# A second head group whose exponentials VectorE transposes in 32x32 blocks and TensorE multiplies as 32x32 array tiles

## The reference, cut to what matters

```python
# layer 0, 8 heads of 32
q, k, v = proj(Wq, bq), proj(Wk, bk), proj(Wv, bv)
scores = einsum('bhqd,bhkd->bhqk', q, k) / sqrt(32)
scores = where(adj + eye > 0, scores, -inf)
out = einsum('bhqk,bhkd->bhqd', softmax(scores), v)
h = x + out @ Wo.T + bo
h = (h - mean(h)) * rsqrt(var(h) + 1e-5) * gamma + beta
# layer 1, one head, logits that are a sum of a row and a column term
fp = h @ fc_w.T + fc_b
logits = (fp @ q_w.T + q_b) + (fp @ k_w.T + k_b).T + (1 - adj) * -1e9
y = softmax(leaky_relu(logits)) @ fp + h
```

## Time and profile before

| | |
|---|---|
| time, median of 3 runs | 985.11 us (984.9 to 985.22) |
| the profiled execution | 985.61 us, of which its span 983.4 us |
| TensorE's granted clock, mean over the span | 0.981 |
| busy: PE, PEld, DVE, ACT, POOL | 95%, 79%, 78%, 81%, 31% |
| DMA: moved, mean rate | 112.59 MB, 114 GB/s |

### The profile page before, as it was taken

The page is one execution under the profiler, slowest core; times in us unless marked ns, Lnnn a source line. Parts: engine busy times, 40 slices in busy tenths (PEclk is TensorE's granted clock), DMA queues, the critical chain, the costliest instruction groups (busy, mean ns, idle before and its releaser), DMA issues. The chain is left out here.

```text
span 983.4 us, 22056 instructions
## 1 busy us (share of the span) xinstructions
PE 932.2 (95%) x7432; PEld 777.8 (79%) x7432; DVE 768.7 (78%) x2012; ACT 796.1 (81%) x1900; POOL 300.5 (31%) x408
## 2 busy tenths in 40 slices
PE   4498999999999999999999999999999999999966
PEld 3276888888888888888788888878887888888755
DVE  3287987979788797978878797888879797887832
ACT  2187988989888897988889798988989898897923
POOL 0002332334333233433214243432323343232441
PEclk8699999999999999999999999999999999999988
DMA  5576856666575666657476665737666564756100
GB/s 150 85 110 149 118 141 108 130 119 99 136 116 133 108 130 129 109 126 117 123 119 133 123 129 109 118 124 116 150 111 129 108 108 130 118 120 108 44 22 22
DMA packets 74430, 112.59 MB, mean 114 GB/s; under 512 B 6736, under 2 KB 33360, under 8 KB 74320
## 3 DMA queue, kind: packets, MB, share of 16 engines
q1 hardware_dynamic: 74320, 111.18, 58.8%
HBM read 52.44 MB, written 8.39 MB: 62 GB/s over the span
## 5 line engine op out<-in xcount | busy, mean ns | idle before, releaser
L912 DVE CUSTOM_DVE_ANT_0 sm_bank<-sm_bank,masks 128x512 f32<-128x512 f32 x512 | 352.3, 698 | 124.1 <-PE sm_bank L494 121.2
L679 ACT ACTIVATE e<-sm_bank,row_min 128x512 f32<-128x512 f32 x512 | 355.3, 696 | 41.9 <-DVE row_min L912 41.9
L504 PE MATMUL et_bank<-ident,e 128*128 128x128 f32 x2048 | 307.9, 272 | 3.2 <-DVE e_t L920 1.9
L504 PEld LDWEIGHTS et_bank<-ident,e 128*128 128x128 f32 x2048 | 251.6, 140 | 42.5 <-issue 7.3
L494 PE MATMUL sm_bank<-k_stack,q_stack 96*128 96x512 f32 x512 | 248.0, 485 | 13.5 <-DMA k_stack<-kt_lo 12.7
L671 ACT COPY e_t<-et_bank 128x512 f32<-128x512 f32 x272 | 161.0, 592 | 16.1 <-PE et_bank L504 14.2
L920 DVE COPY e_t<-et_bank 128x512 f32<-128x512 f32 x240 | 164.4, 685 | 11.8 <-PE et_bank L504 10.2
L494 PEld LDWEIGHTS sm_bank<-k_stack,q_stack 96*128 96x128 f32 x512 | 97.2, 190 | 43.5 <-issue 25.5
L443 PE MATMUL o_bank<-e_t,v 128*32 128x256 f32 x2048 | 123.8, 382 | 0.0
L476 PE MATMUL shared<-feat,z 128*128 128x256 f32 x512 | 121.6, 381 | 0.8 <-ACT z L621 0.8
L679 ACT ACTIVATION_READ_ACCUMULATOR e<-sm_bank,row_min 128x1 f32 x512 | 106.9, 209 | 0.0
(11 more groups left out here) (110 smaller groups left out, 1578.9 us busy)
## 6 DMA issues: line engine op xcount, KB each, us to landing
adj_in<-in_adj SPq DMA_DIRECT2D x32, 1024.0 KB, 5.3
q_stack<-qt_hi SPq DMA_DIRECT2D x64, 256.0 KB, 7.1
k_stack<-kt_hi SPq DMA_DIRECT2D x64, 256.0 KB, 7.2
x_in<-in_x SPq DMA_DIRECT2D x16, 512.0 KB, 6.4
q_stack<-qt_lo SPq DMA_DIRECT2D x32, 256.0 KB, 7.1
k_stack<-kt_lo SPq DMA_DIRECT2D x32, 256.0 KB, 11.1
h<-in_x SPq DMA_DIRECT2D x16, 512.0 KB, 3.9
out_y<-h SPq DMA_DIRECT2D x32, 256.0 KB, 6.8
```

Source lines behind the costliest of these rows:

```text
L504: last = nc.tensor.transpose(et_bank[n % TURNED][:, c * P:(c + 1) * P], e[:, n % ROOM, c * P:(c + 1) * P], ident[:, :])
L679: nc.scalar.activation(e[:, k, :], sm_bank[n % SCORED][:, :], ACT.Exp, scale=-1.0, bias=row_min[:, k:k + 1], accum_out=row_sum[:, g, qt, i ...
L912: nc.vector.tensor_tensor_reduce(bank[:, :], bank[:, :], mask[b % 2][:, qt * N:(qt + 1) * N], 1.0, -LOWEST, ALU.add, ALU.min, row_min[:, k ...
```

## The change

- The tiles of group 1 are no longer transposed on PE and copied from PSUM. `BLOCK` = 2 slots after its scores, DVE transposes each of them from `e` to `e_t` in blocks of 32x32 (`turn_blocks`, one instruction for 128x512). A block stays in its strip of 32 partitions: the strip then holds keys, and the 32 queries of the strip lie along the row.
- The products of group 1 (`pv2`, `pv3`) become `times_v_blocks`: 128 float32 products each, with 32 rows (keys), 32 columns (one head) and 128 moving columns. Each takes one 32x32 tile of the array, and eight consecutive ones take eight different tiles. The four query strips go to four banks: the two transpose banks, `o_bank` and one shared bank. Their key order needs v in every strip, so four transfers on SP's queue (`v4`, 256 KB each) spread it to `v_blocks` once a batch.
- `o_normal` of group 1 becomes four instructions of 128 columns. `turn` of a batch's first two tiles now waits for it.
- The mask (`make_mask`) and the normalising (`normal_rows`) go to GpSimd. `finish` is split: ACT divides by the row sum into `z`, GpSimd adds `z` to h.
- `TURN` goes from 3 to 4, `ROOM` from 4 to 6, DVE copies 4 of the remaining 16 transposed tiles and ACT 12. All tables and the order within a slot are new.

```diff
+HALF = TILES // NG
-TURN = 3
-ROOM = 4
+TURN = 4
+ROOM = 6
+BLOCK = 2
-DVE_COPIED = (0, 3, 5, 6, 13, 14, 15, 18, 22, 24, 25, 26, 27, 28, 29)
+DVE_COPIED = (0, 7, 8, 11)
...
 PE_AT = {
+    "at3": 64, "pv2": 33, "rb1": 35, "pv3": 36, "v1": 4, "xt0": -26, "op0": 39, "op1": 40, "xt1": -23, "k0": -21,
+    "q0": -20, "ht1": 46, "ht0": 46, "fc1": 48, "fc0": 49, "kb": 50, "pv0": 18, "v0": -11, "q1": -11, "pv1": 23,
+    "k1": -8, "et0": 56, "rb0": 25, "et1": 59, "at0": 59, "et2": 59, "at1": 61, "et3": 62, "at2": 63}
...
 DVE_AT = {
+    "rc1": 32, "o_n1": 36, "x_lo0": -26, "h_add0": 39, "stats0": 40, "h_add1": 40, "stats1": 40, "moments": 40,
+    "x_lo1": -23, "k_lo0": -20, "q_lo0": -19, "h_lo1": 46, "h_lo0": 46, "rc0": 17, "q_dot1": 49, "q_dot0": 49,
+    "l_max0": 50, "l_max1": 50, "q_lo1": -10, "k_lo1": -8, "l_recip": 60, "o_n0": 29}
...
 def tile(s):
-    return s // (TILES // NG), s // 2 % GH, 2 * (s // (TILES // PAIRS) % 2) + s % 2
+    if s < HALF:
+        return 0, s // 2 % GH, 2 * (s // (TILES // PAIRS)) + s % 2
+    return 1, (s - HALF) // NT, s % NT
...
+        v_blocks = sb("v_blocks", [P, NT, NT, P])
+        o_quarter = [*et_bank, o_bank, bank_of["pv2"]]
...
+            def spread_values(b):
+                sp.wait_ge(act_done.sem, act_done.all("v", b))
+                sp.wait_ge(pe_done.sem, pe_done.of("pv3", b - 1))
+                for quarter in range(GH):
+                    sp.dma_start(v_blocks[quarter * DH:(quarter + 1) * DH, :, :, :], v[:, :, P:2 * P]).then_inc(v_spread.sem, 16)
...
+            def times_v_blocks(half, b):
+                pe.wait_ge(blocks_turned.sem, blocks_turned.of((half + 3) * (TILES // PAIRS) - 1, b))
+                if half == 0:
+                    pe.wait_ge(v_spread.sem, v_spread.of("v4", b))
+                    pe.wait_ge(act_copied.sem, act_copied.of(max(u for u in range(HALF) if u not in DVE_COPIED), b))
+                    pe.wait_ge(dve_copied.sem, dve_copied.of(max(u for u in range(HALF) if u in DVE_COPIED), b))
+                    pe.wait_ge(dve_done.sem, dve_done.of("o_n0", b))
+                    pe.wait_ge(*bank_read("pv2", b))
+                blocks = e_t[:, half, :, :, :].rearrange("p k g n -> p (k g n)").rearrange("p (h q c n) -> p h q c n", h=2, q=NT, n=DH)
+                for kt in range(NT):
+                    for a in range(NT):
+                        for quarter in range(GH):
+                            rows_in = slice(quarter * DH, (quarter + 1) * DH)
+                            for j in range(2):
+                                o = (2 * half + j) * DH
+                                last = nc.tensor.matmul(
+                                    o_quarter[quarter][o:o + DH, 0:P].rearrange("d (q n) -> d q n", q=NT),
+                                    v_blocks[rows_in, a, kt, o:o + DH], blocks[rows_in, j, :, kt * NT + a, :],
+                                    start=(kt == 0 and a == 0), stop=(kt == NT - 1 and a == NT - 1))
...
             def turn(u, b):
                 pe.wait_ge(exp_done.sem, exp_done.of(u, b))
+                if u < TURNED:
+                    pe.wait_ge(dve_done.sem, dve_done.of("o_n1", b - 1))
...
+            def turn_blocks(u, b):
+                dve.wait_ge(exp_done.sem, exp_done.of(u, b))
+                dve.wait_ge(pe_done.sem, pe_done.of(f"pv{u // (TILES // PAIRS) - 2}", b))
+                nc.vector.transpose(blocks_to(u), e[:, (TILES * b + u) % ROOM, :].rearrange("p (t k a) -> p t a k", t=NT, a=NT))\
+                    .then_inc(blocks_turned.sem, 1)
...
+            def divide(half, b):
+                    last = nc.scalar.activation(z[:, c, 0:D], bank_of[f"at{c}"][:, k * D:(k + 1) * D], ACT.Identity,
+                                                scale=l_recip[:, c:c + 1])
...
+            def finish(half, b):
+                    last = nc.gpsimd.tensor_tensor(h[b % 2][:, c, :], h[b % 2][:, c, :], z[:, c, 0:D], ALU.add)
```

More of the change, by code:

```diff
@@ L124, in all @@
         return max(self.of(step, b) for step in self.place if step[:-1] == name and step[-1].isdigit())
-FILLS = [name for name, _ in steps(PE_AT) if not name.startswith("pv") and name not in ("at1", "at3")]
+FILLS = [name for name, _ in steps(PE_AT) if name not in ("pv0", "pv1", "pv3") and name not in ("at1", "at3")]
 BANK = {
-    "at2": 1, "k1": 0, "v0": 1, "op0": 0, "op1": 1, "v1": 1, "xt0": 1, "xt1": 0, "q0": 0, "ht0": 0, "ht1": 1, "k0": 1,
-    "fc0": 0, "fc1": 1, "kb": 0, "q1": 0, "et0": 0, "et1": 0, "at0": 0, "et2": 1, "et3": 0, "rb0": 1, "rb1": 1}
+    "at2": 0, "k1": 1, "v0": 0, "op0": 1, "op1": 0, "v1": 0, "xt0": 0, "xt1": 1, "q0": 0, "ht0": 0, "ht1": 1, "k0": 1,
+    "fc0": 0, "fc1": 1, "kb": 1, "q1": 1, "et0": 0, "et1": 1, "at0": 0, "pv2": 1, "et2": 1, "et3": 1, "rb0": 0, "rb1": 0}
 BANK["at1"], BANK["at3"] = BANK["at0"], BANK["at2"]
@@ L308, in iteration @@
                 for s in range(TILES):
+                    if (b := due(SP_AT, "store0", s, t)) is not None:
+                        store(0, b)
+                    if (b := due(SP_AT, "v4", s, t)) is not None:
+                        spread_values(b)
+                    if (b := due(SP_AT, "store1", s, t)) is not None:
+                        store(1, b)
+                    if (b := due(SP_AT, "x_again", s, t)) is not None:
+                        for half in range(2):
+                            sp.wait_ge(stored[half].sem, stored[half].of(f"store{half}", b - 2))
+                        sp.dma_start(h[b % 2][:, :, :], rows(x, b)).then_inc(h_loaded.sem, 16)
                     if (b := due(SP_AT, "adj", s, t)) is not None and b > 0:
-                        sp.wait_ge(dve_done.sem, max(dve_done.all("mask", b - 1), dve_done.all("l_max", b - 2)))
+                        sp.wait_ge(pool_done.sem, pool_done.all("mask", b - 1))
+                        sp.wait_ge(dve_done.sem, dve_done.all("l_max", b - 2))
                         sp.dma_start(adj_in[:, :, :], rows(adj, b)).then_inc(adj_loaded.sem, 16)
+                    if (b := due(SP_AT, "stack0", s, t)) is not None:
+                        stack(0, b)
                     if (b := due(SP_AT, "x", s, t)) is not None and b > 0:
@@ L319, in iteration @@
                         stack(1, b)
-                    if (b := due(SP_AT, "store1", s, t)) is not None:
-                        store(1, b)
-                    if (b := due(SP_AT, "store0", s, t)) is not None:
-                        store(0, b)
-                    if (b := due(SP_AT, "x_again", s, t)) is not None:
-                        for half in range(2):
-                            sp.wait_ge(stored[half].sem, stored[half].of(f"store{half}", b - 2))
-                        sp.dma_start(h[b % 2][:, :, :], rows(x, b)).then_inc(h_loaded.sem, 16)
-                    if (b := due(SP_AT, "stack0", s, t)) is not None:
-                        stack(0, b)
             sp.wait_ge(setup_pe, 7)
@@ L525, in iteration @@
+                    if (b := due(PE_AT, "q1", s, t)) is not None:
+                        project_qk("q", WQ, 1, b)
+                    if (b := due(PE_AT, "pv1", s, t)) is not None:
+                        times_v(1, b)
                     if (b := due(PE_AT, "k1", s, t)) is not None:
                         project_qk("k", WK, 1, b)
+                    u, off = ago(s, TURN)
+                    if on(t, off) and u < HALF:
+                        turn(u, t + off)
+                    if (b := due(PE_AT, "at3", s, t)) is not None:
+                        attend(3, b)
@@ L542, in iteration @@
                         fc_project(1, b)
[L543 to L551 removed]
+                    if (b := due(PE_AT, "pv0", s, t)) is not None:
+                        times_v(0, b)
@@ L657, in recips @@
                 copy(recip_wide[g][:, :], f"rb{g}", bank_of[f"rb{g}"][:, :], b)
-            def normal_rows(half, b):
-                act.wait_ge(pool_done.sem, pool_done.of("shift", b))
-                for c in range(2 * half, 2 * half + 2):
-                    last = nc.scalar.activation(h[b % 2][:, c, :], h[b % 2][:, c, :], ACT.Identity, bias=shift[:, c:c + 1],
-                                                scale=rstd[:, c:c + 1])
-                last.then_inc(act_done.sem, 1)
             def copy_turned(u, b):
@@ L686, in iteration @@
+                    u, off = ago(s, TURN)
+                    if on(t, off) and u < HALF and u not in DVE_COPIED:
+                        copy_turned(u, t + off)
+                    if (b := due(ACT_AT, "fin1", s, t)) is not None:
+                        divide(1, b)
                     if (b := due(ACT_AT, "x_hi0", s, t)) is not None:
@@ L968, in iteration @@
-                    if (b := due(DVE_AT, "moments", s, t)) is not None:
-                        combine(b)
                     if (b := due(DVE_AT, "k_lo0", s, t)) is not None:
@@ new lines, in iteration @@
+                    if (b := due(POOL_AT, "mask1", s, t)) is not None:
+                        make_mask(1, b)
```

(10 more changed lines are left out.)

441 lines of the change are left out of this document (225 added, 216 removed), and 24 rows, old and new, of tables (ACT_AT, DVE_AT, PE_AT, POOL_AT).

## The result

The changed kernel takes 1205.9 us (1198.8 to 1209.2), the kernel before 985.0 beside it: a ratio of 1.223 [1.217, 1.229]. The forecast was 946 us in a range of 934 to 1030, so sign and range are both wrong. The profiled execution took 1198.8 us with a span of 1197.1, at a mean granted clock of 0.922 (0.981 before).

The account below looks back on a forecast made before the run. PE was taken to set the pace: 56.7 - 7.0 + 3.6 = 53.3 us a period, plus 0.5 for unevenness; 15 periods 2.9 us shorter, plus 4 us at the ends, gave 946 us, range 934 to 1030.

Parts of the forecast that it names:

- The issuing need not bind: PE, `pv2` and `pv3`: 16 instructions must start every 0.109 us, 7 ns each; a burst showed under 5 ns each.
- rival 3: PE's instruction fetches too slow for 512 a step: about 1020 us at 6.4 us a step, 1240 at 13.8; chance 0.08.
- charged SP's queue with nothing: SP's queue: `v4` adds one MB a batch where 7 move, but `pv2` is 45 us away; no time charged.
- charge of 0.5 us for uneven work: DVE's work falls unevenly over the slots against PE's: 0.5 us a period, ends 0 and 2.
- Eight tiles side by side, rounds of 0.109 us, a step of 3.5: PE, `pv2` and `pv3`: 32 rounds each, 3.75 us with edges in place of 1.95, +3.6 us a batch.
- Rival 1: PE, `pv2` and `pv3`: small tiles run four, not eight, at a time; period 60.3 us, 1043 us in all; chance 0.08.
- rival 2: PE: a floor between starts of products, 0.027 us, makes a step 6.9 us; 1032 us in all; chance 0.07.
- 16 tiles of transposes gone, 7.0 us: PE: 16 tiles of four transposes removed, 0.436 us a tile, 7.0 us less a batch.
- DVE's transpose at 0.60: DVE: each of 16 block transposes a batch costs 0.60 us as a copy does, 9.6 in all; bounds 0.35 and 1.15.
- rival 4: DVE's transpose slow, or DVE otherwise the bound: at 1.15 us each DVE has 56.8 us, up to 1010 us in all; chance 0.12.
- Masks on GpSimd at 1.4 each: GpSimd: two masks of 1024 columns a batch at about 1.4 us each, 2.8 us, on the least loaded engine.
- The ends, +4: After the last scores nothing overlaps: longer `pv3`, `o_n1`, last division and addition, and normalising add 4 us.

Follow-up runs that it names:

- later stacks: The changed kernel with SP's transfers of group 1's stacks waiting for the last step of products (`pv3`) of the batch before: 1104.2 us, ratio 1.120.
- short products: The changed kernel with 32 moving columns instead of 128 in each new product: 1218.5 us; with SP's stack transfers also made to wait, 1124.4 us.
- plain copy: DVE's block transpose replaced by a copy of the same 512 elements, in the changed kernel with half the products and SP's stack transfers delayed: 961.0 us.

## Why the prediction was wrong

**The step that failed** is the one in the change on PE that read "The issuing need not bind", and took 3.75 us from "what the burst and the independent strips show". It asked how close instructions can start and not how fast they are brought. It was named as rival 3, *Instructions do not arrive fast enough*, with 0.08. Its upper price, 1240 us, is near the result by another working: not a steady 27 ns each, but 13.6 ns each from block to block (the steps with later stacks: 5.4 and 6.0 us; the rival had 6.4 from "3 us" a fetch), plus one pause a batch of 5 to 9 us, for a fetch that stands behind 1.5 MB of stack transfers. The rival's lower price, about 1020, left out the second. But with the stacks later, and the steps no longer than it said, the time was 1104 and not 1020; the rest is in the sum below. That a fetch could stand behind the stacks was in view: the page gave 62 packets for 240 instructions each, and the changed table puts `stack1` at the end of an iteration (it waits for the last scores), with `pv2` at slot 1 of the next. I had charged SP's queue with nothing, because I asked only whether its own transfers land in time.

The Trainium skill bears on it in "Runtime: NRT & Kernel Launch", section "Instruction fetch mechanics": PE's instructions come in blocks of 256 over the engine's own DMA queue, ahead of use, and crossing a border is "mostly hidden". The block of 256 agrees with the pauses, and the fetch ahead with the order of packets and borders, which shows one block. "Mostly hidden" holds in before (no wait for issue at the products) and fails here: 123.8 us.

**How the 221 us come together.** The later stacks give back 102. Halving the products on top gives back 107; short products in the same place give back nothing (20 us more, at a lower clock), so this is mostly supply and little array time. What remains, 12 us, is above before although half the products are gone. These steps depend on their order, and are no clean sum.

By the period: 69.70 - 56.74 = +12.96 us. The two steps are 11.52 + 5.50 - 2 x 1.55 = +13.9, the dropped transposes -7.0, and +6 remain outside of them. The distances from each start on PE to the next show where, in means of a period: products with v +14.2 with their edges, transposes -6.7, scores 10.3 to 14.5, that is +4.1, everything else +1.4. Of the scores' 4.1, the 16 tiles of group 1 have 3.2 (5.2 to 8.4). The half clock has little part in it: with the stacks later the granted clock is 0.99 between 160 and 900 us (0.94 in after), and these 16 tiles still take 8.4 us; with half the products on top 8.3, and with the plain copy 7.4. So the prediction's charge of 0.5 us for uneven work, "both ends: 0 and 2", is mis-sized as well. The dearer transposes are shown to be a part of it; the rest stays open.

**Point by point.**
- *Eight tiles side by side, rounds of 0.109 us, a step of 3.5:* right. Eight starts in 0.05 us, rounds of 0.11; the shortest step took 3.79 with its stall. Rival 1 is refuted. (The step at which it sees no gain left comes out at 5.3 us by its own sum, not 5.2.)
- *A floor between starts (rival 2):* refuted for small tiles on different parts of the array: neighbours start 7 ns apart in the first rounds. Its sum has a slip: a floor of 25 ns in place of 27 would take 0.5 us off each of two steps, some 15 us in all and not 8. The 25 ns of the Trainium skill's "TensorE: Matmul & The Clock Gate", section "Wait — 56ns, not 53.3ns?", cited ahead, don't hold here.
- *16 tiles of transposes gone, 7.0 us:* right in count and price (1024 at 274 ns shown).
- *DVE's transpose at 0.60:* mis-sized. It measured 1.04 from start to start, near the upper bound of 1.15, so +7 us a batch on DVE. This, rival 4, is the second cause, though at 1.05 it had foreseen "no change". With supply eased and half the products, the kernel with the transposes took 997.4 and the one with a plain copy 961.0.
- *Masks on GpSimd at 1.4 each:* mis-sized, 3.64, and hidden, as GpSimd stays the least busy.
- *`v4` and SP's queue cost nothing:* wrong for the queue. For `v4` itself it wasn't tried.
- *The ends, +4:* from the last scores to the end it is 62.4 us where it was 51.6, +11; the last `pv2` and `pv3` stall too (5.05 and 7.12 us, 1.55 each before).
- *Granted clock:* no term of the sum allows for a lower one. It fell from 1.00 to 0.50 in the long pause shown, and the mean is 0.922.

With little shortage of instructions left (2.6 us) and half of the products, 997.4 us were measured at the transposes' real price. So 946 would probably have failed without the shortage too, though that kernel has the later stacks besides, and no run takes the shortage alone away. No run that computes the whole beats before.

## What to carry to other kernels

Count instructions, not only their time: a burst of small products needs its instructions from memory, here 256 for each 3.5 us, and it is paid at once when a burst holds more than the one block that was fetched ahead. Where a burst can't be avoided, keep large transfers away from it: one wait on SP gave back 102 us. And an operation that no row shows deserves its upper bound in the sum when the engine it lands on has less than that bound to spare.

## What the runs showed of the hardware that was not expected

- In before, cut into pieces of 64 columns, 32 steps waited 7.2 us for issue, in pieces of 32 with twice the instructions 109.0 us. The one block that is ready ahead, worked out above from packets and borders, fits both: the first burst has 256 instructions, the second 512. In these two runs a packet starts 2.8 us before PE crosses its border at the earliest, and a block beyond the next is never there.
- Eight 32x32 tiles in rows and columns of the array run side by side, 7 ns from start to start.
- DVE's 32x32 block transpose of 128x512 float32 takes 1.13 us, a copy of the same size 0.71.
- GpSimd needs 3.64 us to make a 128x1024 bf16 mask from float32; DVE took 0.68.
- With three quarters of the new products' columns gone the granted clock fell from 0.922 to 0.849, and with the stacks later from 0.968 to 0.881.
